# Reordering the head of a non-local attention kernel, with the small weights' transfer issued behind ScalarE's table load

## The reference

```python
q = jnp.einsum('oc,bcn->bon', Wq, xf) + bq[None, :, None]      # 32 x 1024
k = jnp.einsum('oc,bcn->bon', Wk, xf) + bk[None, :, None]      # 32 x 1024
v = jnp.einsum('oc,bcn->bon', Wv, xf) + bv[None, :, None]      # 256 x 1024
attn = jax.nn.softmax(jnp.einsum('bqi,bqj->bij', q, k), axis=-1)
out = jnp.einsum('bcj,bij->bci', v, attn) + x
```

## Time and profile before

| | |
|---|---|
| median of 3 runs | 163.89 us |
| the profiled execution's own time | 163.81 us |
| its span (first to last instruction) | 162.0 us |
| TensorE busy | 97% of the span |
| VectorE, ScalarE, GpSimd busy | 83%, 67%, 37% |
| TensorE's granted clock over the span | 1.000 |

### The profile page before, as it was taken

The page is one execution under the profiler, slowest core; times in us unless marked ns, Lnnn a source line. Parts: engine busy times, 40 slices in busy tenths (PEclk is TensorE's granted clock), DMA queues, the critical chain, the costliest instruction groups (busy, mean ns, idle before and its releaser), DMA issues.

```text
span 162.0 us, 2456 instructions
## 1 busy us (share of the span) xinstructions
PE 157.5 (97%) x788; PEld 132.3 (82%) x788; DVE 133.9 (83%) x215; ACT 109.2 (67%) x200; POOL 60.0 (37%) x68
## 2 busy tenths in 40 slices
PE   7999999999999999999999999999999999999993
PEld 5677887798888887798888897788888898888882
DVE  1899998888988989997989989895989779846952
ACT  3679887969999545827999646736896655756400
POOL 4479946256222316348443300342333300124500
PEclk9999999999999999999999999999999999999999
DMA  4576672152103030162711130162320330003003
GB/s 161 187 299 166 243 235 89 31 151 63 55 0 97 1 129 2 37 144 67 268 39 49 54 129 0 37 146 67 121 61 1 97 129 0 0 5 129 0 0 130
DMA packets 7780, 14.67 MB, mean 91 GB/s; under 512 B 1504, under 2 KB 2072, under 8 KB 7768
## 3 DMA queue, kind: packets, MB, share of 16 engines
q1 hardware_dynamic: 6728, 13.46, 25.4%
q0 software_dynamic: 608, 0.80, 2.2%
q10 hardware_dynamic: 432, 0.26, 0.5%
HBM read 4.79 MB, written 4.20 MB: 55 GB/s over the span
## 4 chain that ended last, share of the span: by engine, by line
PE 90%; DMA 2%; ACT 2%; DVE 2%; issue 1%; DVEq 0%
PE acc L1009 32%; PE acc L1015 16%; PE slot L849 11%; PE st L996 9%; PE slot L909 7%; PE slot L1009 5%; DMA small_sb<-small 2%; PE slot L1015 2%; ACT dump L504 2%; PE slot L861 2%; PE slot L866 2%; PE slot L935 1%; DVE negmax L667 1%; PE slot L881 1%; DVE x_lo L632 0%
## 5 line engine op out<-in xcount | busy, mean ns | idle before, releaser
L402 POOL TENSOR_TENSOR w_lo<-w_full,w_hi 128x512 fp32r<-128x512 f32 x21 | 28.0, 1338 | 46.6 <-ACT w_full L542 25.4
L1009 PE MATMUL acc<-w_hi,v_hi 128*128 128x512 f32 x112 | 44.3, 395 | 0.0
L1009 PE MATMUL acc<-w_hi,v_lo 128*128 128x512 f32 x112 | 44.1, 394 | 0.0
L542 ACT ACTIVATE w_full<-st 128x512 f32<-128x512 f32 x62 | 36.8, 594 | 7.6 <-PE st L996 7.5
L504 ACT ACTIVATE dump<-slot,negmax 128x1024 f32<-128x1024 f32 x29 | 32.5, 1119 | 10.5 <-DVE negmax L667 10.1
L667 DVE TENSOR_REDUCE negmax<-slot 128x1 f32<-128x1024 f32 x29 | 35.2, 1217 | 2.7 <-PE slot L909 2.7
L1015 PE MATMUL acc<-w_lo,v_hi 128*128 128x512 f32 x112 | 37.4, 396 | 0.0
L734 DVE TENSOR_TENSOR w_lo<-w_full,w_hi 128x512 fp32r<-128x512 f32 x43 | 30.7, 719 | 3.6 <-issue 0.5
L1009 PEld LDWEIGHTS acc<-w_hi,v_hi 128*128 128x128 f32 x112 | 21.1, 189 | 5.0 <-issue 0.2
L1009 PEld LDWEIGHTS acc<-w_hi,v_lo 128*128 128x128 f32 x112 | 21.2, 189 | 4.8
L1015 PEld LDWEIGHTS acc<-w_lo,v_hi 128*128 128x128 f32 x112 | 21.0, 188 | 4.8
(11 more groups left out here) (102 smaller groups left out, 225.2 us busy)
## 6 DMA issues: line engine op xcount, KB each, us to landing
out<-x_sb SPq DMA_DIRECT2D x7, 512.0 KB, 2.8
x_sb<-x SPq DMA_DIRECT2D x3, 1024.0 KB, 5.1
k_b<-k_a SPq DMA_DIRECT2D x8, 192.0 KB, 2.6
q_b<-q_a SPq DMA_DIRECT2D x8, 192.0 KB, 2.6
x_sb<-x SPq DMA_DIRECT2D x2, 512.0 KB, 4.2
k_a<-qk_parts SPq DMA_DIRECT2D x12, 64.0 KB, 2.0
q_a<-qk_parts SPq DMA_DIRECT2D x12, 64.0 KB, 2.2
k_a<-qk_parts POOLq DMA_DIRECT2D x6, 64.0 KB, 2.2
```

The costliest lines, as they stand in the source:

```text
L402: nc.gpsimd.tensor_tensor(w_lo[:, r, :], w_full[:, r, :], w_hi[:, r, :].bitcast(fp32), ALU.subtract).then_inc(w_split_pool, 1)
L542: nc.scalar.activation(w_full[:, r, :], st_home(n), ACT.Exp).then_inc(exp_done, 1)
L1009: nc.tensor.matmul(dst, v[:, b % 2, j, c * P:(c + 1) * P], w_hi[:, n % RING, part], start=(j == 0 and v is v_hi), stop=False)
```

## The change

ScalarE loads its activation table first and issues the small weights' DMA after it. VectorE splits the first piece of the image between `wqk_hi` and `wqk_lo`, and TensorE takes the products of the first piece in the order hi x hi, `x_lo`, `wqk_lo`. The first quarter of q is written by ScalarE (between the two halves of k) and no longer by VectorE, and VectorE makes the low part of k before that of q. TensorE runs 18 idle matmuls, not 20. GpSimd makes `wv_lo` and the first copy of q before `wqk_pair`; it waits for `shift_ready` one quarter of the second image earlier, waits for VectorE's first split of an attention tile before `split_x1(2)`, and does `split_w(1)` before `cut_x1(3)`.

```diff
@@ gpsimd @@
+            pool.wait_ge(wv_cut, 1)
+            nc.gpsimd.tensor_tensor(wv_lo[:, :, :], wv[:, :, :], wv_hi[:, :, :].bitcast(fp32),
+                                    ALU.subtract).then_inc(wv_split, 1)
+            pool.wait_ge(wv_split, 1)
+            put_q_dup(0)
+            pool.wait_ge(q_dup_put, 1)
 
             for half, (parts, made) in enumerate(((wqk_hi, wqk_cut), (wqk_lo, wqk_split))):
...
             pool.wait_ge(pair_made, 2)
-            pool.wait_ge(wv_cut, 1)
-            nc.gpsimd.tensor_tensor(wv_lo[:, :, :], wv[:, :, :], wv_hi[:, :, :].bitcast(fp32),
-                                    ALU.subtract).then_inc(wv_split, 1)
-            pool.wait_ge(wv_split, 1)
-            put_q_dup(0)
-            pool.wait_ge(q_dup_put, 1)
             put_q_dup(1)
...
             cut_x1(0)
             split_x1(0)
             pool.wait_ge(x1_split, 1)
+
+            pool.wait_ge(shift_ready, 1)
             cut_x1(1)
             split_x1(1)
             pool.wait_ge(x1_split, 2)
-
-            pool.wait_ge(shift_ready, 1)
             cut_x1(2)
+
+            pool.wait_ge(w_split_dve, SPLIT_COUNT[0])
             split_x1(2)
             pool.wait_ge(x1_split, 3)
+            split_w(1)
             cut_x1(3)
             pool.wait_ge(x1_cut, 4)
-
-            split_w(1)
             pool.wait_ge(w_split_dve, SPLIT_COUNT[2])
             split_w(3)
@@ scalar @@
+            act.preload_act_table_set("natural_log_exp_and_others")
+
             act.dma_start(small_sb[:, :], small).then_inc(small_in, DMA)
-            act.preload_act_table_set("natural_log_exp_and_others")
...
-            def put_q_hi():
-
-                act.wait_ge(q_lo_put, 1)
-                nc.scalar.activation(q_a[2 * CQK:3 * CQK, Q_PARTS[1]], q_home(1),
+            def put_q_hi(i):
+
+                if i:
+                    act.wait_ge(q_lo_put, i)
+                nc.scalar.activation(q_a[2 * CQK:3 * CQK, Q_PARTS[i]], q_home(i),
                                      ACT.Identity, bias=bias[2 * CQK:3 * CQK, 0:1]).then_inc(q_hi_put, 1)
...
             put_k_hi(0)
+            put_q_hi(0)
             put_k_hi(1)
-            put_q_hi()
+            put_q_hi(1)
             put_q2_full()
@@ vector @@
             nc.vector.tensor_copy(twice(wqk_hi), wqk).then_inc(wqk_cut, 1)
-            dve.wait_ge(wqk_cut, 1)
-            nc.vector.tensor_tensor(twice(wqk_lo), wqk, twice(wqk_hi).bitcast(fp32),
-                                    ALU.subtract).then_inc(wqk_split, 1)
-
             for i in range(4):
                 c, part = piece(i)
+                if i == 1:
+                    dve.wait_ge(wqk_cut, 1)
+                    nc.vector.tensor_tensor(twice(wqk_lo), wqk, twice(wqk_hi).bitcast(fp32),
+                                            ALU.subtract).then_inc(wqk_split, 1)
                 dve.wait_ge(x0_cut, i + 1)
...
-            dve.wait_ge(qk_ready, 1)
-            nc.vector.tensor_scalar(out=q_a[2 * CQK:3 * CQK, Q_PARTS[0]], in0=q_home(0),
-                                    scalar1=bias[2 * CQK:3 * CQK, 0:1], scalar2=None,
-                                    op0=ALU.add).then_inc(q_hi_put, 1)
+            put_k_lo(0)
             put_q_lo(0)
-            put_k_lo(0)
             put_k_lo(1)
             put_q_lo(1)
@@ tensor @@
                 if i == 0:
+
+                    pe.wait_ge(x0_split, 1)
+                    nc.tensor.matmul(dst, wqk_hi[:, c, :], x_lo[:, 0, c, part], start=False, stop=False)
                     pe.wait_ge(wqk_split, 1)
+                    nc.tensor.matmul(dst, wqk_lo[:, c, :], x_hi[:, 0, c, part], start=False, stop=False)
+                    return
...
-            keep_busy(20, QUARTER)
+            keep_busy(18, QUARTER)
```

## The result

| | before | after |
|---|---|---|
| median | 163.86 us (11 runs, 163.71 to 164.11) | 164.27 us (11 runs, 164.19 to 164.64) |
| ratio to before | | 1.0027, 95% interval [1.0017, 1.0036] |
| profiled execution | 163.81 us, span 162.0 | 164.59 us, span 162.8 |
| TensorE, VectorE, ScalarE, GpSimd busy | 97, 83, 67, 37% | 97, 82, 67, 36% |

A forecast was written before the change was run, and what follows sets the result against it. TensorE was taken to bound 90% of the chain, with head delays passing through one for one; 0.12 + 0.32 + 0.03 = +0.47 us gave 164.4 us on the median's scale, range 163.7 to 165.4.

The forecast's parts named there:

- edit 4: GpSimd's new order: tile 1's split stalls TensorE 0.18 us, mostly swallowed by an exponential's wait; +0.03 us, bounds 0 and +0.2.
- Edit 1: Small weights' DMA after the table load: issue waits until 2.06, VectorE starts at 4.98 instead of 4.71 us.
- rival A: The DMA issue doesn't wait for the table load: first products +0.09 us, total 164.3; 0.55 together with the forecast.
- the image's floor: In the head, the image's arrival keeps the first piece's low products from being fed before 6.30 us, +0.09.
- The accumulator's row: On ScalarE, an accumulator read starts at 13.45, before the exponential's end at 13.55: it takes instructions while one runs.
- Edit 2: New order of the first piece on VectorE and TensorE: low products fed at 6.33 instead of 6.21, +0.12 us.
- Edit 3: q's first quarter moved to ScalarE: VectorE waits for k, the first row maximum moves +0.32 us further.
- needed only in the first turn: nothing: GpSimd's later second half of q and second image are wanted only after 19 us, so they cost nothing.
- Edit 5: Two fewer idle matmuls on TensorE end 0.44 us earlier, covered by the wait for wqk_hi; gains nothing.
- B: Small weights land late, VectorE starting at 6.00 us: first products +1.14, total 165.4; chance 0.22.
- C: The two transfers were holding each other up: first products -0.56 us, total 163.7; chance 0.12.
- D: The price of moving q's quarter is wrong, 0.1 instead of 0.32 us: total 164.1; chance 0.11.

The follow-up runs named there:

- idle_20: The changed kernel with 20 idle matmuls instead of 18: 164.53 us, ratio 1.0034 to the kernel before.
- pool_order_only: The kernel before with all of GpSimd's new order alone: 163.87 us, ratio 1.0002 to the kernel before.
- q_on_act_only: The kernel before with only q's first quarter moved to ScalarE and VectorE making k's low part first: 164.58 us, ratio 1.0043.
- ahead_guarded: The kernel before with TensorE's projection products reordered, v's second tile after the first scores, GpSimd's shift_ready wait ahead of cut_x1(1): 164.66 us, ratio 1.0051.

## Why the prediction was right, and where not

- **The direction and the size** were right: +0.41 us measured, +0.47 forecast, and most of it in the step named as the dearest. The nearness of the two numbers owes something to luck: edit 4's term was too small, and no run prices the five edits so that they add up to the median.
- **Edit 1, the small weights.** I took it that the issue waits for the table load (2.06). It doesn't: 0.78, rival A. It mattered little, since the image's floor gave almost the same delay either way. The accumulator's row that I put on the other side was the one to follow, and the trace agrees with what the Trainium skill's "Per-instruction lifecycle" (Perfetto Trace Analysis) has for ScalarE's instructions, that the sequencer goes on to the next one.
- **Edit 2.** Forecast +0.12, of which 0.09 from the floor; measured 0.20 (0.03 to 0.33), and 0.14 in a profile. In the changed kernel's profile the `wqk_lo` product starts at 6.56, not at 6.33; there TensorE, and not VectorE, is late (idle_20). That is also why the first row maximum stands at 11.89 and not at 11.6.
- **Edit 3.** Forecast +0.32; 0.38 in two profiles (3.34 us against 2.96; and 8.55 to 11.89), 0.3 by undoing it. The missing 0.06 is in VectorE's gaps: 9.27 + 0.74 + 0.03 + 0.48 + 0.03 + 0.75, nothing overlaps.
- **Edit 4.** The stall for tile 1 was there (0.20, forecast 0.18). I had it swallowed but for 0.03; in two profiles 0.12 us of it stay, an amount that the medians of pool_order_only (+0.04) neither show nor exclude. The pair of the weights, taken at 1.2 us as in the old trace, took 0.53 in its new place (two casts of 0.29, from 10.31 to 10.84). And "needed only in the first turn: nothing" was wrong as an account of GpSimd's moves. I asked only who waits for GpSimd's results, not what its instructions shut out while they run. Alone the order is worth nothing that can be measured; in the changed kernel it saves 0.34 us by the medians, some 0.2 by the profiles. The step failed without showing in the sum, because the wait for `shift_ready`, which I put at nothing, keeps the two engines apart.
- **Edit 5** gains nothing, as said.
- **Rivals.** B and C, both on the DMA's timing, are out: first cast at 4.77 against 4.71. D is out too: the move costs more, not less.

## What to carry to other kernels

Moving an instruction off a busy engine only gains if that engine has something ready in its place. VectorE gave up 0.5 us of work and waited 0.88 us for a predecessor on ScalarE (q_on_act_only). When a head is shifted, look at the whole stretch behind it for VectorE and GpSimd instructions that now fall on one another; where one of VectorE's is on the path, try to let GpSimd wait for it on a semaphore, even if no data asks for it. Here that was worth some tenths of a microsecond in one shifted head, and in ahead_guarded it moved the collision to another place.

## What the runs showed of the hardware

**VectorE and GpSimd shut each other out on SBUF operands.** In the five rows of VectorE shown above an instruction of VectorE whose operands all lay in SBUF, started while one of GpSimd's ran, took about until that one ended: the 128x4 cast 0.51, 0.48 and 0.39 us for 0.17 to 0.20, the 128x4 subtraction 1.14 for 0.17, the 128x512 subtraction 1.48 for 0.68. Only in the last case did it end clearly later, 0.55 us after GpSimd's, which is a little less than its own 0.68. The other way round, GpSimd's cast that starts at 19.59 in the kernel before, 0.06 us after VectorE's split, took longer than the 0.61 of its like:

```profile
19.59 1.10 POOL L408 CAST x_hi<-x_sb 128x512 fp32r<-128x512 f32 x1
```

VectorE's `v_lo`, which has only one of its inputs in SBUF, kept its 0.68 to 0.69 us beside the same instructions. The Trainium skill (SBUF — State Buffer, "Who interferes with whom") has the rule: a VectorE instruction with two SBUF inputs, or one in a mode that uses both port pairs, and one of GpSimd's that reads SBUF block each other for the whole instruction, whichever starts first. These rows agree; in which mode the 128x4 cast ran, no row shows. I should have set that rule against edit 4.

**ScalarE's queue issued its DMA during the table load**: at 0.78 us in a load from 0.75 to 2.03, and the small weights reach VectorE at 4.77 instead of 4.71.

**Executions differ in when TensorE becomes quick**: products of one shape took 0.77 and 0.79 us, or 0.47 and 0.50, in the same places behind the same instructions. It was worth 0.26 us in the changed head. Why it differs stays open.
